# A rounding stage reworked: weights quantised inside the alignment, magnitudes by pieces, two passes per rounding

## What is computed

```python
def act_qdq(x):                       # one scale for the whole tensor
    qmax = 2.0 ** 15 - 1.0
    scale = jnp.maximum(jnp.max(jnp.abs(x)) / qmax, 1e-12)
    return jnp.clip(jnp.round(x / scale), -qmax - 1.0, qmax) * scale
def fixed_qdq_u16(x):
    return jnp.clip(jnp.round(x * 65536.0), 0.0, 65535.0) / 65536.0
# lpbq_dequant(w): the same to 4 bits, with one scale for each 32 weights of a row
x = act_qdq(x)                                       # 1024 x 128
up = act_qdq(x @ lpbq_dequant(w_up).T)               # 1024 x 384
gate = act_qdq(x @ lpbq_dequant(w_gate).T)           # 1024 x 384
sig = fixed_qdq_u16(jax.nn.sigmoid(gate))
gate = act_qdq(gate * sig)
o = act_qdq(gate * up)
return o @ lpbq_dequant(w_down).T
```

## Time and profile before

| | us |
|---|---|
| median of 3 runs | 2046.13 |
| the runs | 2042.69 to 2058.89 |
| the profiled execution | 2036.04 |
| its span, first to last instruction | 2034.3 |
| PE, DVE, ACT, POOL busy in it | 1654.1, 1327.6, 867.2, 637.9 |

### The profile page before, as it was taken

The page is one execution under the profiler, slowest core; times in us unless marked ns, Lnnn a source line. Parts: engine busy times, 40 slices in busy tenths (PEclk is TensorE's granted clock), DMA queues, the critical chain, the costliest instruction groups (busy, mean ns, idle before and its releaser), DMA issues.

```text
span 2034.3 us, 42486 instructions
## 1 busy us (share of the span) xinstructions
PE 1654.1 (81%) x17607; PEld 1114.2 (55%) x17607; DVE 1327.6 (65%) x2454; ACT 867.2 (43%) x1563; POOL 637.9 (31%) x993
## 2 busy tenths in 40 slices
PE   3003257799877899989998999999987999999999
PEld 1002135467553666556665666656664677777676
DVE  5897766521566778778877778878863555556311
ACT  1000213323233566556565566566553455445332
POOL 0000002000026666666666667667640000000000
PEclk7555689799898999999999999999998999999999
DMA  3000000211004443433433433432321000000011
GB/s 92 19 3 12 0 3 1 59 31 32 3 1 149 112 117 92 107 103 92 114 97 82 114 106 92 126 99 78 93 53 42 1 1 1 1 1 2 25 39 32
DMA packets 73805, 113.39 MB, mean 56 GB/s; under 512 B 16086, under 2 KB 36156, under 8 KB 73582
## 3 DMA queue, kind: packets, MB, share of 16 engines
q1 hardware_dynamic: 72798, 110.43, 19.7%
q10 hardware_dynamic: 816, 0.24, 0.1%
HBM read 83.98 MB, written 27.50 MB: 55 GB/s over the span
## 4 chain that ended last, share of the span: by engine, by line
PE 61%; DVE 27%; ACT 6%; issue 4%; DMA 1%; ACTq 0%; POOL 0%; SPq 0%; DVEq 0%; POOLq 0%
PE PS L1334 8%; PE PS L1062 6%; PE PS L1053 5%; PE PS L2020 4%; PE PS L1523 4%; PE PS L1967 3%; PE PS L1989 3%; PE PS L1571 3%; DVE al_pick L464 3%; PE PS L1437 3%; DVE st_t L1377 2%; DVE st_ss L1382 2%; DVE st_r L1369 2%; PE PS L1463 2%; PE PS L1547 1%
## 5 line engine op out<-in xcount | busy, mean ns | idle before, releaser
L1410 POOL TENSOR_TENSOR st_r<-st_r,st_t 128x512 f32<-128x512 f32 x192 | 243.5, 1272 | 251.8 <-DVE st_t L1377 251.7
L1334 PE MATMUL PS<-st_wqkv,st_xs 128*128 128x512 f32 x576 | 300.7, 606 | 16.3 <-DVE st_xs L1584 9.8
L1425 POOL TENSOR_TENSOR st_r<-st_r,st_gy 128x512 f32<-128x512 f32 x192 | 196.8, 1057 | 3.8
L1369 DVE TENSOR_TENSOR st_r<-PS,st_rot 128x512 f32<-128x512 f32 x192 | 129.8, 676 | 88.5 <-ACT st_sqh L1353 88.3
L2113 DVE TENSOR_REDUCE la_nmx<-PS 128x1 f32<-128x589 f32 x128 | 92.7, 766 | 91.7 <-PE PS L1975 91.7
L2082 ACT ACTIVATE la_p<-PS,la_nmx 128x589 f32<-128x589 f32 x128 | 95.1, 748 | 133.5 <-DVE la_nmx L2113 133.5
L1353 ACT ACTIVATE st_sqh<-PS 128x512 f32<-128x512 f32 x192 | 114.2, 595 | 56.6 <-PE PS L1334 56.6
L1146 DVE SCALAR_TENSOR_TENSOR m_y<-PS,m_g,m_y 128x128 f32<-128x128 f32 x112 | 31.5, 344 | 161.0 <-PE PS L1062 161.0
L1121 ACT ACTIVATE m_h<-PS 128x512 f32<-128x512 f32 x128 | 76.1, 597 | 140.8 <-PE PS L1053 140.8
L1377 DVE TENSOR_TENSOR st_t<-PS,st_rot 128x512 f32<-128x512 f32 x192 | 130.4, 679 | 0.0
L1062 PEld LDWEIGHTS PS<-m_w,m_h 128*128 128x128 f32 x1024 | 121.4, 196 | 16.0 <-issue 16.0
(11 more groups left out here) (314 smaller groups left out, 3530.5 us busy)
## 6 DMA issues: line engine op xcount, KB each, us to landing
st_v_out<-st_v SPq DMA_DIRECT2D x48, 512.0 KB, 2.6
st_vv<-st_v_out SPq DMA_DIRECT2D x96, 256.0 KB, 4.0
st_vv<-st_v_out SPq DMA_DIRECT2D x96, 192.0 KB, 4.8
st_wqkv<-in_st_wqkv SPq DMA_DIRECT2D x18, 512.0 KB, 5.8
m_w<-in_m_w SPq DMA_DIRECT2D x32, 256.0 KB, 3.0
st_vv<-st_v_out SPq DMA_DIRECT2D x72, 64.0 KB, 1.9
st_wo<-in_st_wo SPq DMA_DIRECT2D x6, 512.0 KB
st_w<-in_st_w SPq DMA_DIRECT2D x6, 341.0 KB
```

What stands on the lines that cost most here:

```text
L1334: pe.matmul(PS[:, 2 + m % 2, :], self.xs[:, b, P * t:P * t + P], self.wqkv[:, l % 2, k, 512 * half:512 * half + 512], start=True, stop=Tru ...
L1369: dve.tensor_tensor(h3(self.r[:, t % 2, c, :]), h3(ps), self.rot[:, k, 0, t, :].unsqueeze(1) .broadcast_to([P, 8, D2]), ALU.mult)
L1410: pool.tensor_tensor(r, r, self.t2[:, c % 2, :], ALU.add).then_inc(self.added, 1)
L1425: pool.tensor_tensor(r, r, y[:, 8 * c:8 * c + 8].unsqueeze(2).broadcast_to([P, 8, D2]), ALU.mult)\
```

## The change

- The weights are loaded among the first DMAs of the launch. Ahead of the loads that follow the first ones, SP now waits until `x` and the first constants have landed.
- `weights_dve` (its first four passes) stands in DVE's list between `attend1.kb_dve` and the scan; the rest, `weights_out_dve`, between the scan and `ctx_out_dve`. The clip of the weights is gone. PE's transposes and ACT's copies of them stand after the context's norm. Their buffers are among the alignment's early ones, under `al_path`, so SP and ACT have the transposes behind them before they load it. The walk writes its products into `al_big`, as `al_pick` is dropped.
- The maxima of gate and up are taken by six pieces of 128x512, each as soon as ACT has copied it out, and a reduction of the six.
- The column of maxima is transposed as a 128x128 broadcast, so every partition gets the row; DVE reduces on all partitions. The second reduction on one partition and PE's spreading are gone.
- Each rounding is two passes (`round_dve`, `back_dve`), without the clip. For x and o the second is done in two halves, so that PE can begin after the first.
- PE takes the gate's scale after the first up product, and goes on with the others behind it.
- ACT loads the sigmoid's table ahead of its copies, and in three pieces of 128x1024 takes the sigmoid and rounds it with two more activations (`Identity` with scale and bias). DVE multiplies each piece with one instruction that also clips at 65535/65536.

The diff, cut to its core:

```diff
@@ -331,6 +331,7 @@
                     a, z = max(r0, 1), r1
                     sp.dma_start(self.big[a:z, b, 1:], self.costs[b, SEG + a - 1:SEG + z - 1, :])\
                       .then_inc(self.rows_in, 16)
+            sp.wait_ge(quantised.wT_ready, 3)
             sp.wait_ge(self.enter_ready, 1)
             self.path_load(sp, 0)
 
@@ -349,6 +350,7 @@
             act.wait_ge(self.dist_ready, 2)
             self.skew_load(act, 1)
             self.ctx_act(act)
+            quantised.weights_act(act)
             act.wait_ge(self.enter_ready, 2)
             self.path_load(act, 1)
 
@@ -362,6 +364,7 @@
                           start=False, stop=True).then_inc(self.prod_ready, 1)
             attend1.pe_prepare(pe, 3)
             self.ctx_pe(pe)
+            quantised.weights_pe(pe)
             pe.wait_ge(self.ent_ready, 1)
             pe.transpose(PS[0:KC, 2, 0:B], self.ent[:, :], ident[0:B, 0:B]).then_inc(self.entT_ready, 1)
             for b in range(B):
@@ -422,6 +425,7 @@
             attend1.kv_dve(dve, 3)
             self.ctx_dve(dve)
             attend1.kb_dve(dve)
+            quantised.weights_dve(dve)
             dve.wait_ge(self.skew_in, 2 * SEG * 16)
             shift = [p + 1 if p < 16 and p % SEG < SEG - 1 else 31 for p in range(32)]
             for k in range(STEPS):
@@ -436,6 +440,7 @@
                 dve.tensor_tensor_scan(now[:, 1:], self.low[:, :], self.skew[:, k, :], now[:, 0:1],
                                        ALU.min, ALU.add).then_inc(self.scan_done, 1)
 
+            quantised.weights_out_dve(dve)
             self.ctx_out_dve(dve)
             dve.wait_ge(table_loaded, 16)
             dve.wait_ge(self.rows_in, 64 * len(self.OUT))
...
-        def __init__(self):
...
+        def __init__(self, held):
+            self.wT = sb("q_wT", [P, 3, self.CH, P], at=held)
...
+        def early(self, at):
+            self.wraw = sb("q_wraw", [P, 3, QW], at=at)
+            self.wmax = sb("q_wmax", [P, 3, QW // 32], at=at)
+            self.winv = sb("q_winv", [P, 3, QW // 32], at=at)
...
             order.link(dve, dve.reciprocal(inv, mx))
-            order.link(dve, dve.tensor_tensor(blocks, blocks, inv.unsqueeze(2).broadcast_to([P, G, 32]), ALU.mult))
-            flat = self.wraw[:, :, :].rearrange("p k i -> p (k i)")
+            order.link(dve, dve.tensor_tensor(blocks, blocks, inv.unsqueeze(2).broadcast_to([P, self.G, 32]), ALU.mult))
+
+        def weights_out_dve(self, dve):
+
+            blocks = self.wraw[:, :, :].rearrange("p k (g i) -> p (k g) i", i=32)
+            mx, flat = self.wmax[:, :, :].rearrange("p k g -> p (k g)"), self.wraw[:, :, :].rearrange("p k i -> p (k i)")
             order.link(dve, dve.tensor_scalar(flat, flat, MAGIC, -MAGIC, ALU.add, ALU.add))
-            order.link(dve, dve.tensor_scalar(flat, flat, -8.0, 7.0, ALU.max, ALU.min))
-            dve.tensor_tensor(blocks, blocks, mx.unsqueeze(2).broadcast_to([P, G, 32]), ALU.mult)\
+            dve.tensor_tensor(blocks, blocks, mx.unsqueeze(2).broadcast_to([P, self.G, 32]), ALU.mult)\
                .then_inc(self.w_ready, 1)
 
...
-        def scale_dve(self, dve, j, src):
-
+        def max_dve(self, dve, j, src):
             dve.tensor_reduce(self.mx[:, j:j + 1], src, X, ALU.max, apply_absolute_value=True)\
                .then_inc(self.mx_ready, 1)
+
+        def parts_max_dve(self, dve, j, k, first):
+
+            for i in range(2 * self.CH):
+                c, b = divmod(i, B)
+                dve.wait_ge(self.evac, first + i + 1)
+                order.step(dve.tensor_reduce(self.part[:, i:i + 1], self.h[:, k, c, S * b:S * b + S], X, ALU.max,
+                                             apply_absolute_value=True))
+            dve.wait_ge(order.s, order.at)
+            dve.tensor_reduce(self.mx[:, j:j + 1], self.part[:, :], X, ALU.max).then_inc(self.mx_ready, 1)
+
+        def scale_dve(self, dve, j):
+
             dve.wait_ge(self.mxT_ready, n("dve", self.mxT_ready))
-            dve.tensor_reduce(self.top[:, j:j + 1], PS[0:1, 7, 0:P], X, ALU.max).then_inc(self.top_ready, 1)
-            dve.wait_ge(self.spread, n("dve", self.spread))
-            order.link(dve, dve.tensor_scalar(self.sc[:, j:j + 1], PS[:, 7, P:P + 1], 1.0 / QMAX, 1e-12,
+            order.link(dve, dve.tensor_reduce(self.top[:, j:j + 1], PS[:, 7, 0:P], X, ALU.max))
+            order.link(dve, dve.tensor_scalar(self.sc[:, j:j + 1], self.top[:, j:j + 1], 1.0 / QMAX, 1e-12,
                                               ALU.mult, ALU.max))
             order.link(dve, dve.reciprocal(self.inv[:, j:j + 1], self.sc[:, j:j + 1]))
 
         def scale_pe(self, pe, j):
+
             pe.wait_ge(self.mx_ready, n("pe", self.mx_ready))
-            pe.transpose(PS[0:1, 7, 0:P], self.mx[:, j:j + 1], ident).then_inc(self.mxT_ready, 1)
-            pe.wait_ge(self.top_ready, n("pe", self.top_ready))
-            pe.matmul(PS[:, 7, P:P + 1], const("one")[0:1, :], self.top[:, j:j + 1], start=True, stop=True)\
-              .then_inc(self.spread, 1)
-
-        def quant_dve(self, dve, j, a):
-
+            pe.transpose(PS[:, 7, 0:P], self.mx[:, j:j + 1].broadcast_to([P, P]), ident).then_inc(self.mxT_ready, 1)
+
+        def round_dve(self, dve, j, a):
             order.link(dve, dve.tensor_scalar(a, a, self.inv[:, j:j + 1], MAGIC, ALU.mult, ALU.add))
-            order.link(dve, dve.tensor_scalar(a, a, -MAGIC, QMAX, ALU.add, ALU.min))
-            return dve.tensor_scalar(a, a, -QMAX - 1.0, self.sc[:, j:j + 1], ALU.max, ALU.mult)
+
+        def back_dve(self, dve, j, a):
+            return dve.tensor_scalar(a, a, -MAGIC, self.sc[:, j:j + 1], ALU.add, ALU.mult)
 
         def dve(self, dve):
             up, gate, sig, o = [self.h[:, k, :, :].rearrange("p c t -> p (c t)") for k in range(4)]
             norm.wait(dve, "dve")
             flat = xn[:, :, :].rearrange("p b t -> p (b t)")
-            self.scale_dve(dve, 0, flat)
-            self.quant_dve(dve, 0, flat).then_inc(self.x_quant, 1)
-            dve.wait_ge(self.evac, 6)
-            self.scale_dve(dve, 1, gate)
-            self.quant_dve(dve, 1, gate).then_inc(self.gate_quant, 1)
-            dve.wait_ge(self.evac, 12)
-            self.scale_dve(dve, 2, up)
-            order.link(dve, self.quant_dve(dve, 2, up))
-
-            dve.wait_ge(self.sig_ready, 1)
-            order.link(dve, dve.tensor_scalar(sig, sig, 65536.0, MAGIC, ALU.mult, ALU.add))
-            order.link(dve, dve.tensor_scalar(sig, sig, -MAGIC, 65535.0, ALU.add, ALU.min))
-            order.link(dve, dve.tensor_scalar(sig, sig, 0.0, 1.0 / 65536.0, ALU.max, ALU.mult))
-            order.link(dve, dve.tensor_tensor(gate, gate, sig, ALU.mult))
-            self.scale_dve(dve, 3, gate)
-            order.link(dve, self.quant_dve(dve, 3, gate))
+            self.max_dve(dve, 0, flat)
+            self.scale_dve(dve, 0)
+            self.round_dve(dve, 0, flat)
+            for b in range(B):
+                self.back_dve(dve, 0, xn[:, b, :]).then_inc(self.x_quant, 1)
+            self.parts_max_dve(dve, 1, 1, 0)
+            self.scale_dve(dve, 1)
+            self.round_dve(dve, 1, gate)
+            self.back_dve(dve, 1, gate).then_inc(self.gate_quant, 1)
+            self.parts_max_dve(dve, 2, 0, 2 * self.CH)
+            self.scale_dve(dve, 2)
+            self.round_dve(dve, 2, up)
+            order.step(self.back_dve(dve, 2, up))
+            for c in range(self.CH):
+                dve.wait_ge(self.sig_ready, c + 1)
+                g = self.h[:, 1, c, :]
+                order.step(dve.scalar_tensor_tensor(g, self.h[:, 2, c, :], 65535.0 / 65536.0, g, ALU.min, ALU.mult))
+            dve.wait_ge(order.s, order.at)
+            self.max_dve(dve, 3, gate)
+            self.scale_dve(dve, 3)
+            self.round_dve(dve, 3, gate)
+            order.link(dve, self.back_dve(dve, 3, gate))
             order.link(dve, dve.tensor_tensor(o, gate, up, ALU.mult))
-            self.scale_dve(dve, 4, o)
-            self.quant_dve(dve, 4, o).then_inc(self.o_quant, 1)
+            self.max_dve(dve, 4, o)
+            self.scale_dve(dve, 4)
+            self.round_dve(dve, 4, o)
+            for b in range(B):
+                self.back_dve(dve, 4, self.h[:, 3, :, S * b:S * b + S]).then_inc(self.o_quant, 1)
             for b in range(B):
                 dve.wait_ge(self.down, b + 1)
                 dve.tensor_tensor(x[:, b, :], x[:, b, :], PS[:, b, :], ALU.add).then_inc(x_ready, 1)
 
         def pe(self, pe):
             self.scale_pe(pe, 0)
-            pe.wait_ge(self.x_quant, 1)
             pe.wait_ge(self.wT_copied, 3)
             k = 0
-            for w, j in ((0, 1), (1, 2)):
+            for w in range(2):
                 for c in range(self.CH):
                     for b in range(B):
+                        if k < 2:
+                            pe.wait_ge(self.x_quant, k + 1)
                         if k >= 6:
                             pe.wait_ge(self.evac, k - 5)
```

(22 more changed lines are left out.)

42 lines of the change are left out of this document (21 added, 21 removed).

## The result

| | before | after | 
|---|---|---|
| median, us (runs taken side by side, 4 and 4) | 2044.41 | 2020.78 |
| ratio of the times, 95% interval | | 0.9886 (0.9851 to 0.9921) |
| the profiled execution, us | 2036.04 | 2033.09 |

The median fell by 23.6 us, 1.1% (0.8 to 1.5% by the interval). The forecast was 2018.4 in a range of 2009 to 2029. So the two profiles have to be read by stage, and not by their totals.

A forecast was written before the change was run, and what follows sets the result against it. The quantised stage was taken as a serial chain, mostly DVE passes; PE sets the end from 700 us on. Savings of 8.5 + 7.5 + 1.3 + 5.1 + 5.3 = 27.7 us took the median 2046.13 to 2018.4, range 2009 to 2029.

The forecast's parts named there:

- The weights: Moved out of the stage's head, where they held DVE 6.26 us, into the alignment at no cost there.
- both gaps: DVE's idle places in the alignment, 6.07 us before the scan and 3.32 us after it; both covers gone would cost 5.5.
- The scale chain: From a big reduction's end to its scale: 1.33 us instead of 1.81, 0.48 saved five times.
- Gate: PE's start at 190.7 to rounded gate at 205.1: 14.4 us instead of 21.9, saved 7.5.
- Up: Rounded gate to rounded up: 9.3 us instead of 10.6, saved 1.3, if PE keeps its upper clock.
- six of 0.68: Up's reductions by pieces instead of one of 3.35 us: pieces lose, + 0.7, + 0.24 for the last reduction.
- Sigmoid: DVE's three passes and product, 8.78 us, become three products of 1.22, 3.7 in all; saved 5.1.
- the rival: Table reloads between ACT's sigmoid pieces: 5.9 us after cover, 2024.3, or 2031.2 at 2.66 a switch; chance 0.06.
- Halves of o: o's second pass in halves, PE's first half 0.8 us early; a half 1.0, at worst 1.8.
- The end: PE's start on the last products to the stage's last addition: 7.95 us, unchanged, ending at 245.5.
- The next stages as long as before: Sign of a right forecast; longer later stages would say something outside the stage has moved.
- arrives whole at the end: Premise that the quantised stage's saving, 27.7 us, reaches the end because every later stage waits for its x.

The follow-up runs named there:

- second pair of profiles: Unedited changed kernel and kernel before, each profiled again; changed kernel's median 2021.82, ratio 0.9881; stage 65.4 us against 94.4, stack 967.5 against 955.3.
- undoing any one part: Changed kernel with weights back in the stage, sigmoid's rounding back on DVE, or gate's and up's pieces undone: stage 71.3, 71.1, 71.6 us against 65.9.
- five padding products: Changed kernel plus five 1x1 products early in PE's list (20 instructions), restoring before's list length: median 2014.59, ratio 0.9861 to the kernel before.
- 37 and 32: 1x1 products added to PE's list: 37 in the changed kernel (2011.09, ratio 0.9827), 32 in the kernel before (2039.67, ratio 0.9957).
- more traffic: Changed kernel plus 48 DRAM-to-DRAM copies of 512 KB, one per stack tile, which nothing waits for: median 2019.71, ratio 0.9866.
- less did much: v's copies in the stack cut to 16 of 512 columns: changed kernel 1996.75 (0.9757), kernel before 2023.97 (0.9898).

## Why the prediction was right, step by step

| step, us | predicted | measured |
|---|---|---|
| x: its reduction to PE's start | 3.9 | 3.91 |
| gate: PE's start to rounded | 14.4 | 13.54 |
| up: to rounded | 9.3 | 8.71 |
| sigmoid and product | 3.7 | 3.4 |
| second rounding, o, to PE's last products | 19.4 | 19.6 |
| last products to the last addition's end | 7.95 | 9.20 |
| together | 58.7 | 58.4 |

That the sums agree to 0.3 us is partly luck: gate, up and sigmoid came out 1.8 us cheaper, the two last steps 1.5 dearer.

- **The weights** were right: hidden in both gaps, 5.3 us dearer where they stood before (6.26 with the clip, by the forecast). They landed 5.4 to 5.8 us after issue. The scan began 0.4 us later than 33.5 and x's reduction 1.1 later than 186.8, but not for want of cover. DVE was idle, and PE had begun the last distance products at 21.32 instead of 20.55. In the second pair of profiles the scan begins at 32.16 after and at 32.44 before, and on average the alignment ends at the same time in both kernels (177.6 us, six and four profiles).
- **The scale chain** (1.33) measured 1.28: 220.85 to 222.13. A broadcast transposition was priced rightly by the nearest rows.
- **Gate**: the last of six copies ended 7.8 us after PE's start instead of 8.5, because PE's clock rose earlier in this execution, which the forecast did not have; the six-column reduction is 0.16, where 0.2 was taken.
- **Up**: the term "six of 0.68" was mis-sized. Independent pieces follow each other every 0.59, so pieces lose only 0.3. The forecast's prices of a product, 0.96 and 1.9 at the two levels, were a little high: ACT's copies of the gate in before start 1.71 us apart at first and 0.86 later, one behind each product. PE kept its clock over the short pause, as forecast; without the pieces it doesn't.
- **Sigmoid**: three products at 1.16, not 1.22. ACT was ready at 215.8, half a microsecond before DVE wanted the third. No table load between the pieces: the rival falls, as the Trainium skill has it ("ScalarE: Activation LUTs", "Table sets: the hidden batching unit"). Of the same page's 2.66 us for a switch the trace shows only 1.28; 215.79 to 217.10 lie between the activations on either side.
- **Halves of o** take 2.47 together, the first 1.3, between the 1.0 taken and the bound of 1.8; PE's start is 0.2 late by it.
- **The end** was the largest miss of the stage: "unchanged" was wrong. Twelve products take 8.46 us instead of 7.23, at a mean clock of 0.63 instead of 0.74, though in neither kernel does PE wait for DVE once it has begun. Every profile with the whole change shows it (7.9 to 8.5 us) and none of before (7.2 to 7.3); undoing any one part brought it back to 7.0 to 7.6. Both bursts start at the lower level after an almost idle stretch; what lets one rise sooner, I can't tell.
- **"The next stages as long as before"** is the step that failed. The windows of the 16.8 us behind the stage, before (length, then busy us and count of PE, PEld, DVE, ACT, POOL, then the clock) and after:

```profile
273.20:290.00 16.80, 12.26 (x43) 6.49 (x42) 7.55 (x12) 4.35 (x7) 0.23 (x1) 0.90 0.03 8
```

```profile
246.20:263.00 16.80, 13.18 (x43) 7.26 (x42) 6.67 (x11) 4.18 (x6) 0.23 (x1) 0.80 0.03 8
```

The clock is 0.80 instead of 0.90, and the stages up to the second context attention are 1.1 us longer on average (338.0 against 336.9). The stage itself took 94.45 on average of four profiles with before's stage and 65.9 of six with the changed one: 28.5 less, 27.4 with the stages behind, against 27.7 forecast. The medians show 23.4 and 23.6. With PE's list as long in both kernels it is 28.4 (five padding products, 1 less 0.9861; 23 to 34) and 26.7 (37 and 32). So the sum was right for what it covers, and some 4 us are missing behind it. What failed is the premise that a saving in this stage "arrives whole at the end": in both profiles of after the stack behind it is longer, by more pauses of PE at late blocks and by the lower clock after them. The blocks begin 20 instructions earlier, which is the likeliest reason. The profiles overstate how much. The profiled executions of after lie 12, 5 and 16 us above their medians (the third with more traffic), so the 12 to 18 us of the stack are not the loss of a typical execution. That the place moves the time is shown by the padding; that it makes all of the 4 us is not, since the intervals are about as wide as that.

The last stages, 473.5 or 478.5 us with either kernel, are the clock too: in every profile of 473.5 the lower level costs 5.1 us of them, in every one of 478.5 it costs 10.2. So the 5.0 us of the first table don't belong to the change.

**What stays open**: why a block in a burst of data is late in one case and not in another (more traffic in all did nothing, less did much), and what makes PE's clock stay low longer in one execution of the same kernel than in the next.

## What to carry to other kernels

In a stage that is one serial chain, rows of the nearest shape gave a sum of 58.7 us where 58.4 were measured, each step within 0.9 us but the last. Bursts of an engine whose clock falls when it idles are the exception: the same twelve products cost 1.2 us more after the change, so don't carry their old time over. What is saved reaches the end only up to the noise of the long stages behind; compare them by stage, in more than one profile, and split each into PE's idle time and the cost of its lower clock, before a loss is laid to the change. And a change in the number of instructions is a change of its own: pad the list and time it again before you judge one per cent.

## What the hardware showed

- The instruction queue moves 16 KB blocks over the same DMA engines as data (141 packets, 2.31 MB). PE pauses for up to 5 us when a block is late, in this kernel mostly where 128 small products run in 1.5 us, and resumes 1.2 to 1.8 us after it has landed. 118 of 125 late blocks landed while the DMA engines were over half busy.
- A pause costs more than itself: behind the one of 3.96 us the granted clock was 0.50 over 2.7 us. Over the stack the lower level cost 15.4 us in one execution of before and 29.0 in one of after.
- Padding of 148 instructions moved a median from 2021.8 to 2011.1 (ratios 0.9881 and 0.9827 to before in their own sets).
- DVE reduces 128x512 in 0.69 us alone, and begins one every 0.59 when they wait for nothing.
- A two-scalar DVE pass over 128x3072 takes 1.82, over three strided pieces of 128x512 1.3: two such halves, one behind the other, take 2.47, 0.65 more than the whole.
